# Third attention: the values of the first batch and a fifth chunk are projected ahead of the first scores

## The reference

```python
q = (x @ Wq.T + bq).reshape(b, l, 32, 16).transpose(0, 2, 1, 3)
k = (x @ Wk.T + bk).reshape(b, l, 32, 16).transpose(0, 2, 1, 3)
v = (x @ Wv.T + bv).reshape(b, l, 32, 16).transpose(0, 2, 1, 3)
scores = jnp.einsum('bhqd,bhkd->bhqk', q, k) / math.sqrt(16)
scores = jnp.where(causal, scores, -jnp.inf)
att = jax.nn.softmax(scores, axis=-1)
out = jnp.einsum('bhqk,bhkd->bhqd', att, v)
x = _layernorm(x + (out.transpose(0, 2, 1, 3).reshape(b, l, 512) @ Wo.T + bo))
```

## Time and profile before

| | us |
|---|---|
| timed, median of 3 | 2073.86 |
| profiled execution, its own time | 2077.2 |
| span of that execution | 2075.3 |
| PE busy | 1918.8 (92%) |
| DVE busy | 1145.2 (55%) |
| ACT busy | 843.4 (41%) |
| POOL busy | 845.6 (41%) |
| third attention, entry | 1376.4 |
| its first scores | 1393.6 |
| its step 0 | 1424.1 |
| its step 1 | 1439.1 |

### The profile page before, as it was taken

The page is one execution under the profiler, slowest core; times in us unless marked ns, Lnnn a source line. Parts: engine busy times, 40 slices in busy tenths (PEclk is TensorE's granted clock), DMA queues, the critical chain, the costliest instruction groups (busy, mean ns, idle before and its releaser), DMA issues.

```text
span 2075.3 us, 29630 instructions
## 1 busy us (share of the span) xinstructions
PE 1918.8 (92%) x10936; PEld 1278.0 (62%) x10936; DVE 1145.2 (55%) x2195; ACT 843.4 (41%) x1855; POOL 845.6 (41%) x1363
## 2 busy tenths in 40 slices
PE   6899977999999999999998898969999897999897
PEld 3454435888888888888886787834444454544343
DVE  4666465666666666666667324135556354566345
ACT  1556523444444444444444333313555403565420
POOL 2455315645455555554554444412444312343301
PEclk9899978999999999999999999989999998999998
DMA  7233000101010101010000224043333006111101
GB/s 199 35 45 105 2 10 1 51 1 51 1 51 1 52 1 52 1 52 15 37 31 1 107 92 172 32 53 41 62 60 93 30 1 78 33 38 49 45 0 41
DMA packets 46209, 94.59 MB, mean 46 GB/s; under 512 B 7689, under 2 KB 35721, under 8 KB 43145
## 3 DMA queue, kind: packets, MB, share of 16 engines
q1 hardware_dynamic: 43474, 90.34, 17.2%
q10 hardware_dynamic: 2592, 2.36, 0.8%
HBM read 61.68 MB, written 2.10 MB: 31 GB/s over the span
## 4 chain that ended last, share of the span: by engine, by line
PE 78%; DVE 11%; ACT 4%; issue 3%; DMA 2%; POOL 1%; ACTq 0%; POOLq 0%; SPq 0%; DVEq 0%
PE PS L1373 9%; PE PS L1454 9%; PE PS L452 5%; PE PS L555 5%; PE PS L1873 5%; PE PS L533 5%; PE PS L499 5%; PE PS L580 4%; PE PS L1432 3%; PE PS L1384 3%; PE PS L1886 3%; PE PS L1416 3%; PE PS L1844 2%; PE PS L467 2%; PE PS L501 2%
## 5 line engine op out<-in xcount | busy, mean ns | idle before, releaser
L973 ACT ACTIVATE PB<-PS 128x512 f32<-128x512 f32 x480 | 281.0, 599 | 240.8 <-PE PS L533 237.9
L749 DVE TENSOR_REDUCE NM<-PS 128x2 f32<-128x1024 f32 x192 | 209.2, 1091 | 185.9 <-PE PS L501 184.9
L878 POOL TENSOR_SCALAR_AFFINE_SELECT PB<-PB 128x256 f32<-128x256 f32 (+1 forms) x480 | 174.2, 367 | 322.6 <-ACT PB L973 316.5
L499 PE MATMUL PS<-KQ 96*128 96x512 bf16 (+3 forms) x768 | 189.6, 312 | 46.0 <-DMA KQ<-LOW 31.5
L533 PE MATMUL PS<-KQ 99*128 99x512 bf16 (+3 forms) x768 | 183.9, 305 | 5.5 <-DMA KQ<-NMT 2.5
L1771 POOL TENSOR_SCALAR PR<-PR,RCP 128x512 f32<-128x512 f32 (+3 forms) x256 | 135.4, 539 | 106.7 <-DVE RCP L1569 106.5
L1582 DVE TENSOR_REDUCE NX<-PS 128x1 f32<-128x512 f32 (+3 forms) x256 | 124.8, 488 | 77.5 <-PE PS L1405 71.7
L452 PE MATMUL PS<-XTT,WA 128*128 128x512 f32 x288 | 146.9, 617 | 13.4 <-DVE ident_masks_b L2411 11.9
L501 PE MATMUL PS<-ident_masks_b 128*128 128x128 bf16 x768 | 151.7, 226 | 0.0
L1640 ACT CAST OTH<-PS 128x512 fp32r<-128x512 f32 x64 | 37.6, 587 | 280.5 <-PE PS L1437 280.5
L499 PEld LDWEIGHTS PS<-KQ 96*128 96x128 bf16 x768 | 77.4, 101 | 116.1 <-issue 57.9
(11 more groups left out here) (306 smaller groups left out, 4578.6 us busy)
## 6 DMA issues: line engine op xcount, KB each, us to landing
KQ<-HI SPq DMA_DIRECT2D x90, 128.0 KB, 4.0
KQ<-MID SPq DMA_DIRECT2D x72, 128.0 KB, 4.8
WB<-f_w SPq DMA_DIRECT2D x12, 768.0 KB, 4.5
WB<-w1o SPq DMA_DIRECT2D x8, 1024.0 KB, 7.8
WC<-f_w SPq DMA_DIRECT2D x10, 768.0 KB, 4.4
WB<-w1a SPq DMA_DIRECT2D x8, 768.0 KB, 4.3
WB<-w1b SPq DMA_DIRECT2D x8, 768.0 KB, 5.8
WA<-w SPq DMA_DIRECT2D x6, 1024.0 KB, 6.4
```

What stands on the lines that cost most here:

```text
L499: pe.matmul(ps, KQ[0:SR, self.query(G, h), i * P:(i + 1) * P], KQ[0:SR, self.key(G, h), 0:n], start=True, stop=False)
L749: x = dve.tensor_reduce(nm[:, h:h + 2, i], PS[:, b:b + 2, 0:(i + 1) * P], AX.X, ALU.max, negate=True)
L878: pool.affine_select(blocks, blocks, [[0, count], [1, P]], ALU.is_ge, 0.0, base=0, channel_multiplier=-1).then_inc(s16["probs_ready"].sem, 1)
L973: act.activation(PB[:, n % PBS, :], PS[:, 4 + n % 2, :], ACT.Exp, scale=self.scale)\
```

## The change

The 16 value matmuls of batch 0 and the four of chunk 4 are moved from between the first scores to ahead of them, after the barrier. Chunk 5 then takes the places behind units 0 to 3 of G = 0, chunk 6 those of G = 1, and chunk 7 alone remains in step 0. The takes and splits on DVE, ACT and POOL move with them. No instruction is added or taken away.

```diff
--- before.py
+++ after.py
@@ -586,11 +586,8 @@
             def aside(self, pe, s, k):
 
 
-                if self.wide and s == 0:
-                    if k < 4:
-                        self.project(pe, 6, k)
-                    elif 5 <= k < 9:
-                        self.project(pe, 7, k - 5)
+                if self.wide and s == 0 and k < 4:
+                    self.project(pe, 7, k)
                 first = 1 if self.wide else 6
                 if s in self.late and first <= k < first + NC:
                     self.project(pe, self.late[s], k - first)
@@ -629,6 +626,13 @@
                             self.project_v(pe, 0, t, c)
                     for c in range(NC):
                         self.project(pe, 3, c)
+                else:
+                    for t in range(NT):
+                        for c in range(NC):
+                            self.project_v(pe, 0, t, c)
+                    for c in range(NC):
+                        self.project(pe, 4, c)
+                    self.aux = on["v_ready"].sem, on["v_ready"].at(3)
                 for G in range(2):
                     for a in range(6):
                         self.scores(pe, G, a)
@@ -637,17 +641,8 @@
                         if not self.wide:
                             if G == 0 and 1 <= a <= 4:
                                 self.project(pe, 4, a - 1)
-                        elif G == 0:
-                            self.project_v(pe, 0, a // 2, 2 * (a % 2))
-                            self.project_v(pe, 0, a // 2, 2 * (a % 2) + 1)
-                        elif a < 2:
-                            self.project_v(pe, 0, 3, 2 * a)
-                            self.project_v(pe, 0, 3, 2 * a + 1)
-                        else:
-                            self.project(pe, 4 + (a - 2) // 2, 2 * (a % 2))
-                            self.project(pe, 4 + (a - 2) // 2, 2 * (a % 2) + 1)
-                if self.wide:
-                    self.aux = on["v_ready"].sem, on["v_ready"].at(3)
+                        elif a < 4:
+                            self.project(pe, 5 + G, a)
 
                 for s in range(last):
                     more = s + 2 < last
@@ -783,6 +778,7 @@
                 elif self.wide:
                     for m in range(4):
                         self.take(dve, m)
+                        self.take_v(dve, 0, m)
                 else:
                     for m in range(3):
                         self.take(dve, m)
@@ -791,10 +787,8 @@
                 for G in range(2):
                     for a in range(6):
                         self.maxima(dve, G, a)
-                        if self.wide and (a % 2 == 1 if G == 0 else a == 1):
-                            self.take_v(dve, 0, a // 2 if G == 0 else 3)
-                        if self.wide and G == 1 and a in (3, 5):
-                            self.take(dve, 4 if a == 3 else 5)
+                        if self.wide and (a == 1 or G == 1 and a == 5):
+                            self.take(dve, 4 + G if a == 1 else 6)
                         if self.rope and G == 1 and a in (0, 2, 4):
                             self.turn(dve, 4) if a == 0 else self.take(dve, 2 + a // 2)
                     if G == 0 and not self.wide and not self.rope:
@@ -806,8 +800,6 @@
                         self.beside(dve, st, s, a)
                     if s:
                         self.norm(dve, st, s - 1)
-                    if s == 0 and self.wide:
-                        self.take(dve, 7)
                 if self.wide:
                     self.tails[0].finish(dve, NT - 1)
                 self.norm(dve, st, last - 1)
@@ -821,8 +813,10 @@
                 t = s - self.out_step
                 if self.rope and a == 1 and s - 2 in self.late:
                     self.take(dve, self.late[s - 2])
-                if a == 2 and self.wide and s in (0, 1, 2):
-                    self.take(dve, 6) if s == 0 else self.take_v(dve, 1, 2 * s - 2)
+                if a == 3 and self.wide and s == 0:
+                    self.take(dve, 7)
+                if a == 2 and self.wide and s in (1, 2):
+                    self.take_v(dve, 1, 2 * s - 2)
                 if a == 2 and not self.wide and s - 1 in self.late:
                     self.turn(dve, self.late[s - 1]) if self.rope else self.take(dve, self.late[s - 1])
                 if a == 2 and not self.wide and s == 4:
@@ -893,23 +887,23 @@
                     self.low(pool, 2)
                     self.rotate(pool, 3)
                 else:
-                    for m in range(4):
+                    for m in range(5 if self.wide else 4):
                         self.low(pool, m)
                 self.split_max(pool, 0)
                 if self.rope:
                     self.rotate(pool, 4)
                     self.low(pool, 3)
-                self.low(pool, 4)
+                self.low(pool, 5 if self.wide else 4)
+                self.split_max(pool, 1)
                 if self.wide:
-                    self.low(pool, 5)
-                self.split_max(pool, 1)
+                    self.low(pool, 6)
                 for s in range(last):
                     if s and s + 1 < last:
                         self.split_max(pool, s + 1)
                     for k in range(10):
                         self.causal(pool, s, k)
-                        if s == 0 and k == 6 and self.wide:
-                            self.low(pool, 6)
+                        if s == 0 and k == 7 and self.wide:
+                            self.low(pool, 7)
                         if self.rope and k == 5 and s - 1 in self.late:
                             self.rotate(pool, self.late[s - 1])
                         if self.rope and k == 5 and s - 2 in self.late:
@@ -918,8 +912,6 @@
                             self.low(pool, self.late[s - 1])
                         if k == 5 and 0 <= s - self.out_step - 1 < NT:
                             self.tails[0].root(pool, s - self.out_step - 1)
-                    if s == 0 and self.wide:
-                        self.low(pool, 7)
                     b, t = divmod(s, GROUPS)
                     if 2 <= t < 6 and self.bo is not None:
                         if s == 2:
@@ -1003,15 +995,18 @@
                 elif not self.wide:
                     self.high(act, 4)
                     self.middle(act, 4)
+                else:
+                    for m in (4, 5):
+                        self.high(act, m)
+                        self.middle(act, m)
                 self.take_max(act, 0)
                 if self.rope:
                     self.high(act, 4)
                     self.middle(act, 3)
                     self.middle(act, 4)
                 elif self.wide:
-                    for m in (4, 5):
-                        self.high(act, m)
-                        self.middle(act, m)
+                    self.high(act, 6)
+                    self.middle(act, 6)
                 for s in range(last):
                     for k in range(10):
                         self.exp(act, s, k)
@@ -1028,10 +1023,10 @@
                         if k == 4 and self.rope and s - 2 in self.late:
                             self.middle(act, self.late[s - 2])
                         if s == 0 and self.wide:
-                            if k in (3, 8):
-                                self.high(act, 6 if k == 3 else 7)
-                            if k in (4, 9):
-                                self.middle(act, 6 if k == 4 else 7)
+                            if k == 4:
+                                self.high(act, 7)
+                            if k == 6:
+                                self.middle(act, 7)
                         if k == 6 and self.wide and s in self.late:
                             self.high(act, self.late[s])
                         if k == 5 and 0 <= s - self.out_step - 2 < NT:
```

## The result

The changed kernel takes 2057.58 us (median of 4, 2056.27 to 2061.17) against 2073.24 (median of 4, 2071.07 to 2073.97). The ratio is 0.9931, interval 0.9918 to 0.9944. Its profiled execution took 2056.27 us, span 2054.2. I forecast 2056.5 within 2053.8 to 2060.8.

The account below looks back on a forecast made before the run. PE bounds the kernel except while idle for a transfer at the third attention's entry. 17.6 us moved, 2.6 clock and 1.1 old stalls, less 0.4, 0.5 + 1.7 + 1.5 and 0.2, give 17.4: 2073.86 to 2056.5, range 2053.8 to 2060.8.

Parts of the forecast that it names:

- The prefix: Third attention's entry: the values of batch 0 and chunk 4 fill PE's idle hole, 17.6 us at the hot clock.
- the 0.4 us late start: The third attention's first scores start at 1394.0 instead of 1393.6, behind the work moved ahead of them.
- First scores: Third attention, units 0 to 11: 14.1 us, ending at 1408.1, 16.0 us earlier, with one 0.5 us wait on DVE.
- Step 0 and the late load: Third attention: step 0 lasts 12.1 us with a 1.6 us exponential stall; the maxima load then delays step 1 by 1.5.
- the sum's first number: Start of the third attention's step 1 before the change, 1439.1, set against 1421.7 after it: 17.4 us earlier.
- my own layout: Schedule of the third attention's engines laid out from the entry at 1376.4, putting step 1's start at 1421.7.
- the 0.2 that I called rounding: 0.2 us counted against the gain in the sum of terms for the third attention.
- A: The clock falls in the third attention's new stalls: gain 13 to 16 us, time 2059.5, chance 30%.
- B: The maxima load for the third attention's step 1 isn't late: gain 18.9 us, time 2055.0, chance 14%.
- C: The third attention's first scores wait on DVE more than laid out, 2.4 us: time 2058.9, chance 6%.
- D: Value matmuls wait at the third attention's entry and run only from 1393.6: 2072 to 2075 us, chance 2%.
- E: PE runs cold from the third attention's entry on: step 1 20 us late, 2094 us, chance 2%.

Follow-up runs that it names:

- experiment 1: The kernel before, with 20 extra matmuls with overwritten results in PE's idle time at the third attention's entry, no work moved: 2070.06 us.
- experiment 7: Changed kernel timed again (2055.49 us), with step 1's maxima load and chunk 6's middle part reordered (2054.06), and with the first attention's load also early (2053.20).
- experiment 4: The changed kernel with chunk 5 also ahead of the first scores, chunk 6 in G = 0, 7 in G = 1, none in step 0: 2060.83 us.
- experiment 2: The changed kernel with only the values ahead; chunks 4 and 5 between the first scores, 6 and 7 in step 0: 2061.55 us.
- experiment 6: The changed kernel with chunk 6's middle part on ACT behind step 0's second exponential, POOL's low part moved with it: 2058.66 us.
- experiment 3: The kernel with only the values ahead, plus four extra matmuls with overwritten results behind them, before the first scores: 2059.16 us.

## Why the prediction was right, and where it was off

- **What bounds.** PE idle for a transfer, full behind it. Right: the work moved into the hole is gone from behind it, and experiment 1 parts the clock from the work.
- **The prefix.** 17.6 us forecast, 17.27 measured, at clock 1.00 all the way; the 0.4 us late start didn't come. DVE's takes delayed nothing: the second value take ended at 1380.0, the third chunk take began at 1380.42.
- **First scores.** 14.1 forecast, 14.45 measured, one wait on DVE (0.5 and 0.37).
- **Step 0 and the late load.** Step 1 starts 45.3 us after the entry in the forecast, 45.12 measured. The stall on the exponentials was 1.6 and is 1.54; the small ones are 0.76 where I had 0.1; the load's wait is 1.18 for 1.5. ACT's exponential started 0.02 us behind the 1.28 us table load again (1408.07 behind 1406.77), so the drain that the Trainium skill ("ScalarE: Activation LUTs", section "What ACT_TABLE_LOAD costs") adds to a switch did not show, and ACT's instruction ahead of the load ended 0.02 us before it. The fixed cost of 2.0 us that the prediction quotes for a transfer stands in a section on transfers that GpSimd issues; here SP issues them, and no term of the sum uses it.
- **The mis-sized step is the sum's first number, "Step 1 began at 1439.1".** That row is the second `scoresT` of step 1, not the first. The first is the last of these three:

```profile
1437.68 0.60 PE L533 MATMUL PS<-KQ 99*128 99x256 bf16 x3
1438.11 0.38 PE L499 MATMUL PS<-KQ 96*128 96x512 bf16 x1
```

  It starts near 1437.9. With the right mark my own layout gives 1437.9 - 1376.4 - 45.3 = 16.2 us, and 0.3 more as step 1's old stall goes; 16.9 was measured. I forecast 17.4.
- **The same error in the terms.** The waits were forecast well: 1.12 us of old ones go (1.1), 3.85 come (3.7), and the clock gives 2.6 (2.6). That leaves 16.87 - 2.59 - 1.12 + 3.85 = 17.0 for the moved work, where I had 17.6. This 17.0 is a remainder, not a reading. The 0.4 us late start, which didn't come, made up for most of that error, and the 0.2 that I called rounding had nothing behind it.
- **Luck in the time.** The stage moved 16.9, the time 15.7 by the first medians and 18.5 in the later timings of experiment 7 (2073.94 to 2055.49). The range would have held either, but the half microsecond of error in the sum is smaller than this scatter.
- **Rivals.** A (the clock falls in the new stalls) didn't happen: waits of 1.54 and 1.18 us left it at 1.00. Its mechanism is real and near: waits of 2.58, 2.81 and 2.86 us in experiments 4, 2 and 6 were each followed by a stretch at 0.51, 0.50 and 0.60. B (the load isn't late) is false. C, D and E didn't occur; E's premise is false, since PE ran the entry at 1.00 in the changed kernel and in experiment 1.

## What to carry to other kernels

Work that depends on nothing belongs in the hole in front of a transfer, exactly as much as the hole holds: the last piece paid 4.7 us for 3.4 of work because it also kept the clock up, and the next one, past the end of the hole, cost 3.4. After that look at what the earlier start pulls together in the DMA queue, and issue the small urgent transfer ahead of the large patient ones. When two waits follow each other and the second ends at a fixed time, removing the first only lengthens the second; take the second first.

## What the runs showed of the hardware

Removing a stall made the stretch longer: in experiment 6 one wait of 2.86 us in place of 1.54 and 1.18 brought the granted clock down and cost 1.6 us. Matmuls whose results nobody reads gained 2.6 us in experiment 1 and 2.5 in experiment 3 by keeping PE at granted clock 1.00 (2.4 GHz) where it ran at 0.50 (1.2 GHz) without them. A small transfer issued behind row transfers held PE until 1.2 us after the DMA engines had drained (1416.0 to 1417.24 in the changed kernel); issued ahead of the last six it held nothing.
